# A decoder layer on one core: the convolution of two of its four groups from single-pass products of split operands

## What is computed

```python
        kv = vr[:, :, :, None, :] * x2r[:, :, None, :, :]
        k_f = jnp.fft.rfft(k.astype(jnp.float32), n=fft_size)
        y = jnp.fft.irfft(jnp.fft.rfft(kv, n=fft_size) * k_f[None, :, None, None, :], n=fft_size)[..., :L]
...
        out = jnp.einsum('bhijl,bhil->bhjl', y, x1r)
...
    x = _layernorm(x + _L0_attn_ref(x, L0_attn_wq, ...), axis=-1)
    x = _layernorm(x + _L0_xattn_ref(x, L0_xattn_k, fside_S2_0, ctx_2048, ctx_2048, 8), axis=-1)
    x = _layernorm(x + _L0_ffn_ref(x, L0_ffn_gate_W_packed, ...), axis=-1)
```

## Time and profile before

| | us |
|---|---|
| median of three runs | 560.65 (560.31 to 561.21) |
| the profiled execution | 560.49 |
| its span | 558.7 |
| PE busy | 532.1 (95% of the span) |
| DVE busy | 374.2 (67%) |
| ACT busy | 147.3 (26%) |
| POOL busy | 124.4 (22%) |

### The profile page before, as it was taken

One profiled execution on the slowest core, in us unless ns is written; L12 is line 12 of the kernel. 1 busy time (PEld: TensorE's weight loads), 2 busy tenths in 40 slices (PEclk: granted clock), 3 DMA queues, 4 the chain that ended last, 5 costly groups with the idle time before them and its releaser, 6 DMA issues.

```text
span 558.7 us, 8787 instructions
## 1 busy us (share of the span) xinstructions
PE 532.1 (95%) x3351; PEld 432.8 (77%) x3351; DVE 374.2 (67%) x782; ACT 147.3 (26%) x259; POOL 124.4 (22%) x195
## 2 busy tenths in 40 slices
PE   5999989999989999999999999999999999799993
PEld 5766777656878888766888888866888888688883
DVE  3999889977766668875455668874464777632334
ACT  3432320142442112242242111241422002223230
POOL 2100069300003444120003444120014561100001
PEclk9999899989999999999999999999999999899998
DMA  6532322121201110032001110040001100100001
GB/s 175 161 113 78 90 76 86 38 77 39 95 0 39 49 48 19 1 116 74 1 1 38 58 38 20 2 147 6 1 19 48 57 30 0 39 0 2 1 0 39
DMA packets 25258, 26.82 MB, mean 48 GB/s; under 512 B 2816, under 2 KB 22784, under 8 KB 25216
## 3 DMA queue, kind: packets, MB, share of 16 engines
q1 hardware_dynamic: 14208, 15.73, 9.5%
q10 hardware_dynamic: 10576, 8.95, 5.5%
q0 software_dynamic: 432, 1.57, 0.8%
HBM read 24.15 MB, written 2.10 MB: 47 GB/s over the span
## 4 chain that ended last, share of the span: by engine, by line
PE 81%; DVE 9%; issue 3%; DMA 3%; POOL 2%; ACT 1%; ACTq 0%; POOLq 0%; SPq 0%; DVEq 0%
PE bank L1049 17%; PE bank L1051 16%; PE bank L1050 16%; PE front_bank L1181 5%; PE front_bank L1184 4%; PE front_bank L1182 4%; PE front_bank L1118 3%; PE front_bank L1105 3%; PE front_bank L1153 3%; PE front_bank L1049 2%; PE front_bank L1050 2%; PE front_bank L1051 2%; DMA wo_sb<-in_woT 1%; PE front_bank L1129 1%; POOL ve L425 1%
## 5 line engine op out<-in xcount | busy, mean ns | idle before, releaser
L1049 PE MATMUL bank<-x2T_lo,ffn_hi 128*128 128x512 f32 x256 | 111.1, 434 | 3.5 <-DVE inter L991 2.1
L991 DVE TENSOR_TENSOR inter<-bank,inter 128x512 f32<-128x512 f32 x64 | 44.2, 690 | 90.0 <-PE bank L1051 89.7
L1051 PE MATMUL bank<-x2T_hi,ffn_hi 128*128 128x512 f32 x256 | 102.2, 399 | 0.0
L1050 PE MATMUL bank<-x2T_hi,ffn_lo 128*128 128x512 f32 x256 | 101.9, 398 | 0.0
L475 POOL TENSOR_TENSOR qbd<-qT_sb,ctxT_sb 128x256 f32<-128x256 f32 x128 | 79.0, 640 | 69.2 <-PE front_bank L1184 55.8
L425 POOL TENSOR_TENSOR ve<-ve,minus_half 128x2 f32<-128x2 f32 x24 | 17.4, 741 | 296.5 <-DVE ve L792 228.1
L649 ACT ACTIVATE inter_hi<-inter 128x512 fp32r<-128x512 f32 x64 | 40.4, 632 | 147.9 <-DVE inter L991 147.9
L1049 PE MATMUL bank<-ffn_lo,inter_hi 128*128 128x256 f32 x256 | 76.8, 300 | 1.1 <-DVE inter_lo L985 1.1
L643 ACT ACTIVATE inter<-bank 128x512 f32<-128x512 f32 x64 | 38.2, 597 | 136.0 <-PE bank L1051 135.9
L1051 PE MATMUL bank<-ffn_hi,inter_hi 128*128 128x256 f32 x256 | 72.1, 282 | 0.0
L1050 PE MATMUL bank<-ffn_hi,inter_lo 128*128 128x256 f32 x256 | 72.0, 281 | 0.0
(11 more groups left out here) (127 smaller groups left out, 779.5 us busy)
## 6 DMA issues: line engine op xcount, KB each, us to landing
toep_sb<-in_toep ACTq DMA_DIRECT2D x64, 128.0 KB, 2.1
xT_sb<-in_xT SPq DMA_DIRECT2D x4, 512.0 KB, 5.6
ctxT_sb<-in_ctxT SPq DMA_DIRECT2D x4, 512.0 KB, 4.5
x_sb<-in_x SPq DMA_DIRECT2D x4, 512.0 KB, 5.7
ctx_sb<-in_ctx SPq DMA_DIRECT2D x4, 512.0 KB, 6.6
out<-ctxT_sb POOLq DMA_DIRECT2D x3, 512.0 KB, 3.4
raw_w<-in_gate_p SPq DMA_DIRECT2D x8, 128.0 KB
raw_s<-in_gate_s SPq DMA_DIRECT2D x8, 128.0 KB
```

The lines of the kernel that those rows point to most:

```text
L991: nc.vector.tensor_tensor(inter[:, n % 2, :], up_ps[:, :], inter[:, n % 2, :], ALU.mult).then_inc(inter_ready, 1)
L1049: nc.tensor.matmul(ps, w_hi, x_lo, start=start, stop=False, skip_group_check=True)
L1050: nc.tensor.matmul(ps, w_lo, x_hi, start=False, stop=False, skip_group_check=True)
L1051: return nc.tensor.matmul(ps, w_hi, x_hi, start=False, stop=stop, skip_group_check=True)
```

## The change

Groups 1 and 2 (the second and the third) convolve from split operands; groups 0 and 3 keep the three f32 matmuls. For these two groups:

- ACT rounds the channel's filter to `toep_hi` and the two halves of `kv_sb` to `kv_hi` (`round_conv`, three copies of 128x256). `kv_hi` is the tile `xT_hi`, so `split_x` of the following group now waits for the last convolution.
- POOL subtracts for `toep_lo` and for the first half of `kv_lo`, DVE for the second half (`low`, in both engines). Both low tiles lie in place over `toep_sb` and `kv_sb`.
- PE multiplies nine single-pass products in place of three f32 matmuls (`conv_split`). It waits for `toep_lo` and POOL's half ahead of the first six, for DVE's half ahead of the last three. `split_mm` records them under the same lines as the FFN's (1112 to 1114 in the changed kernel).
- The tables move the channels. In group 1, slot 10 has channels 0 and 1, slots 11 to 14 three each, slot 15 two (before: one in slot 10, then three each). Group 2 gets a table of its own, `mid_slots`: the front stages one slot earlier, as in `last_slots`, then the channels over slots 9 to 15 by 2, 3, 2, 3, 2, 2, 2. Group 3's table is as before.

```diff
-        toep_sb = sb("toep_sb", [P, NTOEP, 2 * P])
+        toep_hi = sb("toep_hi", [P, 2, 2 * P], F32R)
...
+            toep_sb = sbe("toep_sb", [P, NTOEP, 2 * P])
+            qbd = sbe("qbd", [P, 4, T])
...
+        toep_lo = sb("toep_lo", [P, NTOEP, 2 * P], F32R)
+        kv_lo = sb("kv_lo", [P, 4, T], F32R)
...
-        qbd = sb("qbd", [P, 4, T])
         q_two = qbd[:].rearrange("p u (k c) -> p u k c", c=S)
         kv_sb = qbd[:, 0:2, :]
+        kv_hi = xT_hi
...
-        slots[10] = [pause, pause, conv[0]]
+        slots[10] = [pause] + conv[0:2]
         for n in range(5):
-            slots[11 + n] = conv[3 * n + 1:3 * n + 4]
+            slots[11 + n] = conv[3 * n + 2:3 * n + 5]
...
+        mid_slots[9], mid_slots[10] = [pause] + conv[0:2], conv[2:5]
+        mid_slots[11], mid_slots[12] = conv[5:7], conv[7:10]
...
+            return 1 <= g <= 2
...
             def x1T(g, _):
                 products(g, 0)
+                low(g, 0)
...
                     products(g, h + 1)
+                    low(g, h + 1)
...
+            def low(g, h):
+
+                if splits_conv(g):
+                    count(pool, toephi_ready, CH, g - 1, h + 1)
+                    nc.gpsimd.tensor_tensor(toep_lo[:, h % NTOEP, :], toep_sb[:, h % NTOEP, :],
+                                            toep_hi[:, h % 2, :].bitcast(F32), ALU.subtract).then_inc(toeplo_ready, 1)
+                    count(pool, kvhi_ready, 2 * CH, g - 1, 2 * h + 1)
+                    nc.gpsimd.tensor_tensor(kv_lo[:, h % 2, half(0)], kv_sb[:, h % 2, half(0)],
+                                            kv_hi[:, h % 2, half(0)].bitcast(F32), ALU.subtract).then_inc(kvlo_pool, 1)
...
+                if splits_conv(g - 1):
+                    count(act, y_mm, 16, g, 0)
...
+                round_conv(g, 0)
+
+            def round_conv(g, h):
+
+                if splits_conv(g):
+                    count(act, ld_toep[h % NTOEP], 16 * CH // NTOEP, g, 16 * (h // NTOEP + 1))
+                    count(act, y_mm, 16, g, h - 1)
+                    nc.scalar.activation(toep_hi[:, h % 2, :], toep_sb[:, h % NTOEP, :], ACT.Copy)\
+                        .then_inc(toephi_ready, 1)
+                    if h == 0:
+                        count(act, v_mm, 2, g, 2)
+                    for kt in range(KT):
+                        count(act, kv_ready, 32, g, 2 * h + kt + 1)
+                        nc.scalar.activation(kv_hi[:, h % 2, half(kt)], kv_sb[:, h % 2, half(kt)], ACT.Copy)\
+                            .then_inc(kvhi_ready, 1)
...
                     load_filter(g, h + NTOEP - 1)
+                if h + 1 < CH:
+                    round_conv(g, h + 1)
...
                     conv_sum(g, h - 1)
+                if h + 1 < CH:
+                    low(g, h + 1)
+
+            def x1T(g, _):
+                low(g, 0)
+
+            def low(g, h):
+
+                if splits_conv(g):
+                    count(dve, kvhi_ready, 2 * CH, g - 1, 2 * h + 2)
+                    nc.vector.tensor_tensor(kv_lo[:, h % 2, half(1)], kv_sb[:, h % 2, half(1)],
+                                            kv_hi[:, h % 2, half(1)].bitcast(F32), ALU.subtract).then_inc(kvlo_dve, 1)
...
+                if splits_conv(g):
+                    conv_split(g, h, n)
+                    return
...
+            def conv_split(g, h, n):
+
+                count(pe, toeplo_ready, CH, g - 1, h + 1)
+                count(pe, kvlo_pool, CH, g - 1, h + 1)
+                t_hi, t_lo = toep_hi[:, h % 2, :], toep_lo[:, h % NTOEP, :]
+                x_hi, x_lo = kv_hi[:, h % 2, :], kv_lo[:, h % 2, :]
+                diag, off = slice(0, P), slice(P, 2 * P)
+                split_mm(fb[h % 2][:, 0:n], t_hi[:, diag], t_lo[:, diag], x_hi[:, 0:n], x_lo[:, 0:n], True, True)
+                split_mm(fb[h % 2][:, n:2 * n], t_hi[:, off], t_lo[:, off], x_hi[:, 0:n], x_lo[:, 0:n], True, False)
+                count(pe, kvlo_dve, CH, g - 1, h + 1)
+                split_mm(fb[h % 2][:, n:2 * n], t_hi[:, diag], t_lo[:, diag], x_hi[:, n:2 * n], x_lo[:, n:2 * n],
+                         False, True).then_inc(y_mm, 1)
```

More of the change, by code:

```diff
@@ L171, in decoder_layer @@
             "ms_ready", "newton_step", "rms_ready", "half_ready", "sk_ready", "x2lo_ready", "inter_ready", "ilo_ready")
+        kvhi_ready, kvlo_pool, kvlo_dve, toephi_ready, toeplo_ready = sems(
+            "kvhi_ready", "kvlo_pool", "kvlo_dve", "toephi_ready", "toeplo_ready")
         shifted, masked, deq_ready, wlo_ready = sems("shifted", "masked", "deq_ready", "wlo_ready")
@@ L226, in decoder_layer @@
         slots[9] = [("norm", 0), pause, ("x1T", 0)]
-        slots[10] = [pause, pause, conv[0]]
+        slots[10] = [pause] + conv[0:2]
         for n in range(5):
-            slots[11 + n] = conv[3 * n + 1:3 * n + 4]
+            slots[11 + n] = conv[3 * n + 2:3 * n + 5]
         last_slots = [[] for _ in range(NT)]
         last_slots[0], last_slots[1], last_slots[2] = scores[0:2], scores[2:5], scores[5:8]
-        for n in range(4, 11):
+        for n in range(4, 10):
             last_slots[n - 1] = slots[n]
+        last_slots[9] = [pause, pause, conv[0]]
         for n in range(3):
             last_slots[10 + n] = conv[5 * n + 1:5 * n + 6]
+        mid_slots = last_slots[0:9] + [[]] * (NT - 9)
+        mid_slots[9], mid_slots[10] = [pause] + conv[0:2], conv[2:5]
+        mid_slots[11], mid_slots[12] = conv[5:7], conv[7:10]
+        for n in range(3):
+            mid_slots[13 + n] = conv[2 * n + 10:2 * n + 12]
         join = [("join", k) for k in range(6)]
@@ L240, in stages @@
         def stages(g, s, third):
-            now = (last_slots if g == G - 1 else slots)[s]
+            now = (slots, slots, mid_slots, last_slots)[g][s]
             cut = ((0, 0, 0, 0), (0, 1, 1, 1), (0, 1, 2, 2), (0, 1, 2, 3), (0, 1, 2, 4), (0, 1, 3, 5))[len(now)]
@@ L270, in ahead, with splits_conv, half @@
             return g == 1
+        def splits_conv(g):
+            return 1 <= g <= 2
+        def half(kt):
+            return slice(kt * NB * CI * CI, (kt + 1) * NB * CI * CI)
         def proj_bank(g, p):
@@ L1018, in _ @@
             schedule(dve, turn, {"score": score, "squares": squares, "rms": rms, "factor": factor, "outproj": outproj, "norm": norm,
-                                 "conv": conv, "join": join, "norm2": norm2}, nothing, inner, split, unpack, finish)
+                                 "x1T": x1T, "conv": conv, "join": join, "norm2": norm2}, nothing, inner, split, unpack, finish)
         @block.tensor
```

## The result

The changed kernel takes **572.25 us** (median of six runs, 569.68 to 575.18) against 560.58 of the kernel before beside it, a ratio of 1.0208 with a 95% interval of 1.0171 to 1.0245. The forecast was 566.2 with a range up to 571.0: the direction was right, the size was not. The profiled execution took 571.59 us, its span is 569.8. In the run with two of three channels split, further down, two executions of six, the profiled one among them, took 1304.71 and 1789.86 us; its figures are those of the other four.

A forecast was written before the change was run, and what follows sets the result against it. PE bounds the kernel, but POOL's longer stream would hold up the split groups: 560.49 plus 4.3 (second group) plus 1.4 (third group) gives 566.2 us, with an 8-in-10 range of 556.5 to 571.

The forecast's parts named there:

- PE's price: On PE, nine single-pass matmuls take 1.07 us instead of 1.30 for an f32 convolution, saving 0.23 us a channel.
- The mechanism: In three-channel slots POOL carries 8.3 us, above the old slot's 8.12, and also waits for ACT's filter rounding.
- The collisions: DVE subtractions delay POOL in three-channel slots: about 0.2 us for each of 256 columns, 0.45 for one of 512.
- Rival 3: POOL stands still for all of DVE's subtractions, 0.41 and 0.68 us; three-channel slot 9.6 us, kernel 572 us; chance 0.12.
- six products on POOL: POOL in a three-channel slot: a pair of products takes 1.21 us, so 0.605 each.
- six subtractions on POOL: POOL in a three-channel slot: each 128x256 subtraction takes 0.605 us, with 0.64 as the other end.
- wait for the rounded filter: In a three-channel slot POOL waits 0.4 us for channel c's filter, which ACT rounds only after inner_hi.
- worked slot: Three channels a, b, c followed through the engines' queues: a steady slot takes 8.67 us against 8.12.
- ACT's copy of 256 columns: On ACT, three such copies per channel: 0.45 us for one and 0.37 from one to the next.
- The third group's earlier front part: Moving the front stages one slot earlier costs nothing, as the fourth group's PE row shows (70.00 of 70.00 us busy).

## Why the prediction failed, step by step

**What was right.** PE's price: split products follow each other in steps of 0.12, as in the earlier trace rows; here are the second and the last of the nine of one channel in the changed kernel, seven steps apart:

```profile
191.06 0.28 PE L1113 MATMUL front_bank<-xT_hi,toep_lo 128*128 128x256 f32 x1
...
191.90 0.28 PE L1114 MATMUL front_bank<-xT_hi,toep_hi 128*128 128x256 f32 x1
```

With no wait the split channel gives back its 0.23 us (7.88 against 8.12 for one a slot, 7.63 for two). The mechanism: POOL becomes the bound of the three-channel slots, with ACT's order added. The collisions: 0.18 us for a DVE subtraction of 256 columns (0.2 forecast) and 0.44 for `inter_lo` (0.45). The Trainium skill, "SBUF — State Buffer", section "SBUF: two separate sides", has the loser blocked for the whole of the other's instruction; the runs show 0.18 and 0.44, where DVE's instructions take 0.41 (the forecast's figure) and 0.68. Rival 3, which that rule says, gave 572, the time that came out, and a slot of 9.6, nearer to 9.41 than the forecast's, by a mechanism that the rows refute: a number that fits proves no cause.

**What failed: two terms of the slot's sum, and one that stood in no sum.** The three-channel slot (8.67 forecast, 9.41 measured):

| term | forecast | measured | difference |
|---|---|---|---|
| six products on POOL | 6 x 0.605 = 3.63 | 3.55 | -0.08 |
| six subtractions on POOL | 6 x 0.605 = 3.63 | 6 x 0.70 = 4.19 | +0.56 |
| wait for the rounded filter | 0.4 | 0.71 | +0.31 |
| collisions | 3 x 0.2 + 0.45 = 1.05 | 3 x 0.17 + 0.44 = 0.96 | -0.09 |

The forecast's terms add up to 8.71, where its worked slot had 8.67.

The subtractions were the largest. "I take 0.605 and keep 0.64 as the other end" was wrong at both ends. 0.605 came from a product of repeated views; 0.64 from halving the 1.27 of 512 columns. Two plain tiles of 256 columns cost 0.70, more than half of 1.27, which would fit a fixed part that halving the longer row had halved too. The format, which I had suspected, costs nothing on POOL either; the operands do.

The second is the wait: the forecast ended `toep_hi` at 6.4 in the slot and POOL at 6.0. With POOL's stream longer, all of PE's parts lie later, and so do `inner` and `inner_hi`; that the wait grew with the stream is read from this order and was not tried apart. Rounding the filter earlier took it away and brought 3.1 us, or 5.4 by the gelu rows.

The third is channel 0. It is rounded in the stage x1T, ahead of the next slot's gelu on ACT. ACT's timeline of the changed kernel there:

```profile
174.73 1.08 ACT L624 ACTIVATE qT_sb<-front_bank 128x512 f32<-128x512 f32 x2 [0.21 <-PE front_bank L1228]
175.70 0.42 ACT L632 ACTIVATE toep_hi<-toep_sb 128x256 fp32r<-128x256 f32 x1
176.21 0.94 ACT L638 ACTIVATE xT_hi<-qbd 128x256 fp32r<-128x256 f32 x2
177.06 0.58 ACT L694 ACTIVATE inter<-bank 128x512 f32<-128x512 f32 x1
```

and in the kernel before:

```profile
175.29 1.09 ACT L590 ACTIVATE qT_sb<-front_bank 128x512 f32<-128x512 f32 x2 [0.21 <-PE front_bank L1165]
176.81 0.60 ACT L643 ACTIVATE inter<-bank 128x512 f32<-128x512 f32 x1 [0.43 <-PE bank L1051]
```

From the copy of x1T to gelu it takes 2.33 us against 1.52 before: a rounding that waits for POOL's products holds gelu, and that slot takes 5.9 us instead of 5.1. Twice 0.81 is 1.6 us; in the runs without channel 0 the slot is back at 5.1. I had priced ACT's copies only by what waits for them, not by what is queued behind them.

Together: in the second group 0.8 for channel 0 and some 3.5 for four slots (38.2 us by the gelu rows against 34.7), less 0.2 in slot 10; in the third 0.8 and 2.5 for the seven slots (54.2 against 51.7). Its three-channel slots took 9.47 and 8.72 where I had 8.7 and 8.0; of the two-channel slots, the two behind them took 7.34 as forecast (7.3), but the last two 6.9 and 7.5 where I had 6.4 and 6.9. That is 7.4, against which this execution was 2.0 us shorter elsewhere; 5.7 + 7.4 - 2.0 = 11.1, by which the two profiled spans differ.

**Smaller steps.** ACT's copy of 256 columns has a mean of 407 ns for the filter and 412 for the products, by ACT's groups, where I had interpolated 0.45 from the earlier trace rows:

```profile
L638 ACT ACTIVATE xT_hi<-qbd 128x256 fp32r<-128x256 f32 x64 | 25.2, 412 | 20.1 <-POOL qbd L507 19.5
...
L632 ACT ACTIVATE toep_hi<-toep_sb 128x256 fp32r<-128x256 f32 x32 | 13.0, 407 | 0.4 <-issue 0.3
```

The Trainium skill's estimate of 0.40, from "VectorE: DVE Perf Modes", section "The TRN2 errata — SBUF-src ops pay a fixed extra latency per instruction", is the better one. By the forecast's own sum it changed under 1 us. The third group's earlier front part cost nothing, as said. PE waited 10.7 us for POOL's half, forecast 13.

**What remains open.** Why two plain operands cost POOL more than two repeated views was not taken further. The version with nineteen channels gains 3.2 us by its ratio where 4.4 were worked out. The gelu rows place most of the difference in the groups' last slot with the turn behind it: 26.69 us in the second group and 26.45 in the third, no less than the 26.46 and 26.43 of the run with channels 1, 4, 7, 10 and 13, where both channels of that slot are plain. So the three channels split there gave nothing back; why is not shown.

## What to carry to other kernels

Work that is handed from the busiest engine to idle ones has two prices: the sum on each engine, and the place in its in-order queue. Removing the sum (one subtraction left out, fewer channels split) left a loss until the place was right as well; with the place right, eight channels gained and nineteen gained more. Price an instruction by a row with its own kind of operands and its own size, not by half of a longer one. Ask of every instruction that waits what is queued behind it, and split only what the slot can take: here nineteen of 32 channels beat all and none.

## What the runs showed of the hardware

- POOL's two-input instruction of 128x256 f32 costs a step of 0.70 us on two plain tiles and about 0.59 on the convolution's repeated views (1.17 for a pair), subtract or multiply, f32 or fp32r result.
- A DVE subtraction of 256 columns beside it costs POOL 0.18 us, one of 512 columns 0.44.
- A late operand can cost PE time without a wait in the view: only the step between two starts shows it (0.48 instead of 0.24).
